# Inverse softmax sums of the third query block made inside the second attention, block 0 normalised ahead of the one-hots, and only the last block inverted in the output stage

## What is computed

```python
xn = _layernorm(x)
x = x + _L0_attn_ref(xn, ...) + _L0_ffn_ref(xn, ...)      # linear attention; 16 experts
xn = _layernorm(x)
x = x + _L1_attn_ref(xn, ...) + _L1_ffn_ref(xn, ...)      # causal windowed softmax attention; routed block
```

```python
attn = jax.nn.softmax(scores, axis=-1)
out = jnp.einsum('bhqk,bhkd->bhqd', attn, v)
return jnp.einsum('bnh,hm->bnm', out, w_out)
```

## Time and profile before

| what | us |
|---|---|
| median of 3 runs (lowest, highest) | 1543.32 (1541.33, 1543.69) |
| the profiled execution, its own time | 1543.52 |
| its span | 1541.8 |
| TensorE busy in it | 1471.3 (95%) |
| VectorE busy | 1029.9 (67%) |
| ScalarE busy | 755.4 (49%) |
| GpSimd busy | 461.0 (30%) |
| mean granted clock of TensorE | 0.981 |

### The profile page before, as it was taken

The page is one execution under the profiler, slowest core; times in us unless marked ns, Lnnn a source line. Parts: engine busy times, 40 slices in busy tenths (PEclk is TensorE's granted clock), DMA queues, the critical chain, the costliest instruction groups (busy, mean ns, idle before and its releaser), DMA issues. The chain is left out here.

```text
span 1541.8 us, 23547 instructions
## 1 busy us (share of the span) xinstructions
PE 1471.3 (95%) x6981; PEld 1062.9 (69%) x6981; DVE 1029.9 (67%) x2939; ACT 755.4 (49%) x1282; POOL 461.0 (30%) x691
## 2 busy tenths in 40 slices
PE   6999999999998999999989999999999998898998
PEld 4778788888776788788855555555555545687776
DVE  5453666666657656887767886665668974578592
ACT  5623556556564544433325555555555562235561
POOL 0000677777610112323221212221212213054062
PEclk9999999999999999999969999999999999999999
DMA  5001222211110334366797405314134017744021
GB/s 185 1 1 70 95 76 75 112 75 75 55 48 7 130 110 125 121 193 197 193 236 282 110 19 120 74 55 120 35 92 120 13 62 208 247 171 155 22 89 14
DMA packets 107124, 161.53 MB, mean 105 GB/s; under 512 B 12352, under 2 KB 63696, under 8 KB 100624
## 3 DMA queue, kind: packets, MB, share of 16 engines
q1 hardware_dynamic: 101868, 153.64, 32.6%
q10 hardware_dynamic: 4516, 5.38, 1.0%
q0 software_dynamic: 640, 1.31, 0.4%
HBM read 117.44 MB, written 42.87 MB: 104 GB/s over the span
## 5 line engine op out<-in xcount | busy, mean ns | idle before, releaser
L2138 ACT ACTIVATE l_pt<-banks 128x1024 f32<-128x1024 f32 (+3 forms) x288 | 218.6, 811 | 140.2 <-PE banks L2013 138.3
L2210 DVE CUSTOM_DVE_ANT_0 stage<-banks,l_edges 128x384 f32<-128x384 f32 (+3 forms) x384 | 201.7, 542 | 73.1 <-issue 71.8
L2050 PE MATMUL banks<-l_pt,l_v 128*64 128x512 f32 (+3 forms) x1152 | 222.0, 507 | 2.0 <-POOL l_pt L2108 2.0
L718 POOL TENSOR_TENSOR ex_hl<-ex_h,ex_hh 128x512 fp32r<-128x512 f32 x128 | 165.6, 1301 | 81.1 <-ACT ex_hh L686 81.0
L2107 POOL TENSOR_TENSOR l_turn<-l_before 128x2 f32<-128x2 f32 x192 | 38.6, 201 | 385.0 <-ACT l_pt L2138 375.4
L751 DVE SCALAR_TENSOR_TENSOR ex_rw<-banks,ex_wb 128x512 f32<-128x512 f32 x128 | 88.3, 691 | 78.9 <-PE banks L75 78.8
L2213 DVE TENSOR_REDUCE l_mx<-banks 128x1 f32<-128x384 f32 (+1 forms) x208 | 113.1, 544 | 39.9 <-PE banks L1991 39.2
L2050 PEld LDWEIGHTS banks<-l_pt,l_v 128*64 128x64 f32 x1152 | 69.3, 138 | 91.4 <-issue 68.2
L686 ACT ACTIVATE ex_hh<-ex_h 128x512 fp32r<-128x512 f32 x128 | 80.9, 632 | 103.6 <-DVE ex_h L759 103.4
L73 PE MATMUL banks<-ex_xlh,ex_wh 128*128 128x512 f32 x256 | 101.7, 397 | 2.0 <-DVE ex_rw L751 2.0
L74 PE MATMUL banks<-ex_xll,ex_wh 128*128 128x512 f32 x256 | 99.8, 390 | 0.0
(11 more groups left out here) (454 smaller groups left out, 3496.9 us busy)
## 6 DMA issues: line engine op xcount, KB each, us to landing
ex_wb<-gates_by_expert SPq DMA_DIRECT2D x16, 1024.0 KB, 4.6
l_v<-layer_v SPq DMA_DIRECT2D x8, 1024.0 KB, 16.9
layer_qk<-qkv_yh SPq DMA_DIRECT2D x30, 256.0 KB, 3.2
layer_qk<-qkv_yl SPq DMA_DIRECT2D x30, 256.0 KB, 3.6
layer_v<-qkv_vs SPq DMA_DIRECT2D x15, 512.0 KB, 5.0
ex_ws<-ew_in SPq DMA_DIRECT2D x16, 384.0 KB, 5.0
l_q<-layer_qk SPq DMA_DIRECT2D x12, 512.0 KB, 7.7
l_k<-layer_qk SPq DMA_DIRECT2D x12, 512.0 KB, 13.3
```

The costliest lines, as they stand in the source:

```text
L718: pool.tensor_tensor(hl[:, k % RING, :], h[:, k % RING, :], raw(hh[:, k % RING, :]), ALU.subtract).then_inc(hl_done, 1)
L2050: last = pe.matmul(bank[h * 2 * HD:(h + 1) * 2 * HD, (qa - b * BT) * P:(qz + 1 - b * BT) * P], v[par][:, kt, h, :], pt[:, step_part(b, j), ...
L2138: act.activation(pt[:, step_part(b, j), :, 0:width], G.banks[:, 2 * slot:2 * slot + 2, 0:width], ACT.Exp, scale=scale).then_inc(p_done, 1)
L2210: dve.tensor_tensor_reduce(cutoff[:, n % 4, 0:width], G.ps[5 + n % MB][:, 0:width], masked, 1.0, NEG, ALU.add, ALU.max, mx[:, h, m, c:c + ...
```

## The change

In the attention's last turn, SyncE waits for the reciprocal, stores the inverses, spreads block 0's and loads block 1's outputs at u = 6 instead of u = 7, ahead of unit 6's store. At u = 7 it loads the sums of block 2 to a new tile `dn2` once unit 6's store has landed, waits for their reciprocal and stores them. VectorE normalises block 0 before the places and one-hots; the one-hots come in four groups of four, with the reciprocal of `dn2` behind the first group and the low parts of block 0 between the others; the chosen numbers come last. ScalarE's copies go two behind steps 6 and 7 and two behind steps 8 and 9. TensorE's picks move from step 8 to step 10, where they stand ahead of the last two value steps.

In the output stage only block 3's sums are loaded and inverted (64 columns per partition in place of 128). SyncE's order becomes: inverses 1, residual 0 and 1, outputs of block 2, wait for the stores, load of the sums, residual 2 and 3, inverses 2, norm vectors, wait for the reciprocal, store of the inverses, residual 4 and 5, outputs of block 3, wait, inverses 3, residual 6 to 15, biases. VectorE waits for the sums and inverts them at tile 3 instead of at the start.

```diff
--- before.py
+++ after.py
@@ -1784,6 +1784,7 @@
     o_out = [G.sem(f"l1_o_out{k}") for k in range(2)]
     den_in, rden, rden_out, z_in, out_o_in, out_o1_in = (
         G.sem("l1_" + n) for n in ("den_in", "rden", "rden_out", "z_in", "out_o_in", "out_o1_in"))
+    den2_in, rden2, rden2_out = (G.sem("l1_" + n) for n in ("den2_in", "rden2", "rden2_out"))
     w_in, w_hi, w_lo, on, ohi = (G.sem("l1_" + n) for n in ("w_in", "w_hi", "w_lo", "on", "ohi"))
     first_in, far_ones = G.sem("l1_first_in"), G.sem("l1_far_ones")
     nm_done, mh_done, cut_done = G.sem("l1_nm"), G.sem("l1_mh"), G.sem("l1_cut")
@@ -1791,7 +1792,7 @@
         "sr_in", "iota", "link", "sel", "pos_mm", "oh", "pick_mm"))
     PR = 4
     LEAD = 37
-    PLACES, PICKS = 4, 8
+    PLACES, PICKS = 4, 10
     MB = 3
     with ExitStack() as stack:
         M = Memory(nc, stack, "l1_")
@@ -1805,7 +1806,7 @@
         wraw = nc.alloc_sbuf_tensor_at("l1_wraw", [P, NC, D], F32, offset=v0_at)
         pt = nc.alloc_sbuf_tensor_at("l1_pt", [P, PR, 2, TB], F32, offset=G.qw_at)
         ob = M.sb("ob", [P, 2, TB])
-        dn = M.sb("dn", [P, 2 * H0 * TB // P])
+        dn, dn2 = M.sb("dn", [P, 2 * H0 * TB // P]), M.sb("dn2", [P, H0 * TB // P])
         sr, junk, same = G.out_o1[:, :, :].rearrange("p g n -> p (g n)"), M.sb("junk", [P, 2, T], BF16), M.sb("same", [P, 2, P])
         count, rank_of, sel = M.sb("count", [P, NT, 6]), M.sb("rank", [P, NT]), M.sb("sel", [P, NT], BF16)
         place, numi, ordi = M.sb("place", [P, NT]), M.sb("numi", [P, NT], I32), M.sb("ordi", [P, SEL], I32)
@@ -1875,13 +1876,17 @@
                     if last and u == NB + 2:
                         sp.wait_ge(o_out[1], 64 * (PAIRS * NB // 2 - 1))
                         sp.dma_start(dn[:, :], sums_of(S.den, 0, 2)).then_inc(den_in, 16)
-                    if last and u == NB + 3:
                         sp.wait_ge(rden, 1)
                         sp.dma_start(sums_of(S.rden, 0, 2), dn[:, :]).then_inc(rden_out, 16)
                         sp.wait_ge(rden_out, 16)
                         spread_inverses(sp, S, 0, G.out_z, z_in)
                         sp.wait_ge(sel_done, 1)
                         sp.dma_start(G.out_o1[:, :, :], S.o[:, TB:2 * TB].rearrange("(g p) t -> p g t", p=P)).then_inc(out_o1_in, 16)
+                    if last and u == NB + 3:
+                        sp.wait_ge(o_out[0], 64 * (PAIRS * NB // 2))
+                        sp.dma_start(dn2[:, :], sums_of(S.den, 2, 3)).then_inc(den2_in, 16)
+                        sp.wait_ge(rden2, 1)
+                        sp.dma_start(sums_of(S.rden, 2, 3), dn2[:, :]).then_inc(rden2_out, 16)
                     if last and u == 2 * NB - 1:
                         G.last_outputs = lambda queue, no=no, pair=i * 2 + par, b=b: store(queue, no, pair, b)
                     else:
@@ -1896,6 +1901,7 @@
             G.o_out = [(o_out[n], 64 * PAIRS * NB // 2) for n in range(2)]
             sp.wait_ge(out_o_in, 16)
             sp.wait_ge(out_o1_in, 16)
+            sp.wait_ge(rden2_out, 16)
 
         assert KEYS % 2 == 0
 
@@ -2171,8 +2177,8 @@
                             output(i - 1, 2 * NB - 1)
                         for at in due(i, position(u, j + 1), last):
                             rows(*at)
-                        if last and u == 2 * NB - 1 and j == len(plans[u % NB].keys) - 2:
-                            for g in range(NC):
+                        if last and u == 2 * NB - 1 and j in (6, 8):
+                            for g in range(j - 6, j - 4):
                                 act.wait_ge(on, g + 1)
                                 act.activation(G.out_oh[:, g, :], G.out_o[:, g, :], ACT.Copy).then_inc(ohi, 1)
                         if last and u == NB + 1 and j < 4:
@@ -2263,11 +2269,13 @@
                 for t, n in todo[upto(position - 1):upto(position)]:
                     rank(t, n)
 
-            def onehots():
+            def places():
 
                 dve.wait_ge(pos_mm, 1)
                 tokens.done(dve.scalar_tensor_tensor(place[:, :], G.ps[6][:, 0:NT], 1.0, sel[:, :], ALU.add, ALU.mult))
-                for t in range(NT):
+
+            def onehots(tiles):
+                for t in tiles:
                     dve.tensor_scalar(onehot[:, t, :], order[:, :], place[:, t:t + 1], None, ALU.is_equal
                                       ).then_inc(oh_done, 1)
 
@@ -2301,15 +2309,21 @@
                         dve.wait_ge(den_in, 16)
                         dve.reciprocal(dn[:, :], dn[:, :]).then_inc(rden, 1)
                     if last and u == 2 * NB - 1:
-                        onehots()
                         dve.wait_ge(z_in, 64)
                         dve.wait_ge(out_o_in, 16)
                         for g in range(NC):
                             dve.tensor_tensor(G.out_o[:, g, :], G.out_z[:, g, :], G.out_o[:, g, :], ALU.mult).then_inc(on, 1)
-                        chosen()
+                        places()
+                        onehots(range(NT // 4))
+                        dve.wait_ge(den2_in, 16)
+                        dve.reciprocal(dn2[:, :], dn2[:, :]).then_inc(rden2, 1)
+                        onehots(range(NT // 4, NT // 2))
                         for g in range(NC):
                             dve.wait_ge(ohi, g + 1)
                             dve.tensor_tensor(G.out_ol[:, g, :], G.out_o[:, g, :], raw(G.out_oh[:, g, :]), ALU.subtract)
+                            if g % 2 == 1:
+                                onehots(range((g + 3) * NT // 8, (g + 5) * NT // 8))
+                        chosen()
 
             looped(dve, PAIRS // 2, body)
 
@@ -2387,7 +2401,7 @@
     BANKS = 6
     with ExitStack() as stack:
         M = Memory(nc, stack, "o1_")
-        dn = M.sb("dn", [P, 2 * H0 * TB // P])
+        dn = M.sb("dn", [P, H0 * TB // P])
         o_at = nc.sbuf_base
         o = [None, G.out_o1] + [M.sb(f"o{b}", [P, NC, TB]) for b in range(2, NB)]
         z = M.sb("z", [P, 2, NC, TB])
@@ -2420,23 +2434,23 @@
             inverses(1)
             residual(0)
             residual(1)
+            values(2)
             for sem, count in G.o_out:
                 sp.wait_ge(sem, count)
-            sp.dma_start(dn[:, :], sums_of(S.den, 2, NB)).then_inc(den_in, 16)
-            sp.wait_ge(rden, 1)
-            sp.dma_start(sums_of(S.rden, 2, NB), dn[:, :]).then_inc(rden_out, 16)
+            sp.dma_start(dn[:, :], sums_of(S.den, NB - 1, NB)).then_inc(den_in, 16)
             residual(2)
             residual(3)
-            values(2)
+            inverses(2)
             sp.dma_start(R.ln[:, 0, :], I["ln1_w"]).then_inc(R.ln_in, 16)
             sp.dma_start(R.ln[:, 1, :], I["ln2_w"]).then_inc(R.ln_in, 16)
-            sp.wait_ge(rden_out, 16)
-            inverses(2)
-            for t in range(BT, 2 * BT):
+            sp.wait_ge(rden, 1)
+            sp.dma_start(sums_of(S.rden, NB - 1, NB), dn[:, :]).then_inc(rden_out, 16)
+            for t in range(BT, BT + 2):
                 residual(t)
             values(3)
+            sp.wait_ge(rden_out, 16)
             inverses(3)
-            for t in range(2 * BT, NT):
+            for t in range(BT + 2, NT):
                 residual(t)
             R.load_biases(sp, I)
 
@@ -2484,10 +2498,11 @@
                 dve.wait_ge(ohi, (b - 1) * NC + g + 1)
                 dve.tensor_tensor(ol[b][:, g, :], o[b][:, g, :], raw(oh[b][:, g, :]), ALU.subtract).then_inc(olo, 1)
 
-            dve.wait_ge(den_in, 16)
-            dve.reciprocal(dn[:, :], dn[:, :]).then_inc(rden, 1)
             for t in range(NT):
                 b, k = t // BT, t % BT
+                if t == BT - 1:
+                    dve.wait_ge(den_in, 16)
+                    dve.reciprocal(dn[:, :], dn[:, :]).then_inc(rden, 1)
                 if b + 1 < NB:
                     normal(b + 1, k)
                 elif k == 0:
```

## The result

| | kernel before | changed kernel |
|---|---|---|
| median, us (14 runs each) | 1543.18 | 1547.29 |
| lowest, highest | 1540.71, 1545.70 | 1540.44, 1552.73 |
| span of the profiled execution | 1541.8 | 1545.2 |
| last unit: places to the output stage's first product | 11.86 | 13.96 |
| output stage: first product to last addition | 58.20 | 61.37 |

The ratio is 1.0028 with a 95% interval of 1.0016 to 1.0040: the changed kernel is 2.5 to 6.2 us slower, 4.3 in the middle. The forecast was +5.0 (1548.3 us, range 1541.0 to 1553.0).

The account below looks back on a forecast made before the run. Transfers were taken as the scarce thing, with TensorE's gaps, ended by VectorE's waits, what could be won. Attention's end +0.8, row 6 +3.5 and clock +0.7 gave +5.0 on 1543.5, or 1548.3 us against the median; range 1541.0 to 1553.0.

Parts of the forecast that it names:

- part 3: Output stage, block 2: residual row 6, queued behind block 3's 2 MB, lands at 1322.4; +3.5 us, bounds +0.2 and +6.2.
- part 4: TensorE's clock after its idle time at the third block: slow products cost +0.7 us, bounds -1.8 and +1.5.
- Part 2: First wait of the output stage: VectorE starts 3 us earlier but waits 3 us for row 2; nothing won at block 1.
- Part 1: Attention's end: earlier inverses, but work between the one-hots and a wait for the third sums; +0.8 us, bounds -0.6 and +2.0.
- (a): Rival, output stage: residual rows 6 and 7 are in time; -4.5 us, so 1538.8 us; chance 0.14.
- point of decision: Output stage: if row 6 has landed by 1315.3, VectorE's cycle alone sets block 2 and the kernel is faster.
- (b): Rival, output stage: block 3's inverses take 3.0 us instead of 5.5, row 6 at 1319.9; it cancels, 1545.0 us; chance 0.24.
- (c): Rival, attention's end: third sums land at 1280, delaying the one-hots and last value steps; +2.0 us, whole 1549.5; chance 0.12.

Follow-up runs that it names:

- first experiment: Changed kernel with only residual tiles 6 and 7 back ahead of block 3's values and inverses; stage 54.63 us, ratio to the kernel before 0.9995.
- second experiment: Changed kernel with only block 2's values back behind the sums and residual tiles 2 and 3; product at -1.77, end 12.08 us, ratio to the kernel before 1.0023.
- rows first with the one-hots together: Changed kernel with residual tiles 6 and 7 ahead of block 3's transfers and all 16 one-hots in one run behind the places; ratio to the kernel before 0.9979.
- the two with batched low parts: Changed kernel, one-hots together, next block's four chunks made at its first tile; rows 6 and 7 ahead of or behind block 3's transfers: 0.9984, 0.9982 of the kernel before.

## Why the prediction was right

**The direction and its cause** (part 3) held: residual row 6, issued behind 2 MB, decides the third block. Forecast: block 2's inverses at 1310.7, row 6 at 1322.4; measured 1310.81 and 1323.45, the stage having started 0.3 us later than the clock of before. The first experiment shows the cause by moving rows 6 and 7 alone. TensorE reached tile 9 not 3.5 but 4.8 us later, counted from the first product: 0.8 from row 6, and 0.5 because the last products of the tile before ran at the low level (0.63 us each in place of 0.40), which I had counted under part 4. In the second execution of each kernel the difference is 2.0 us (37.2 against 35.2). The forecast of 1310.7 has a slip in it: "about 2.0 us earlier" and 1 us for the norm loads make 3.0, so 1311.2, and I wrote 3.5. That it was met within 0.2 us is luck.

**Part 4** was wrong: I set +0.7 us for slow products behind tile 9. Measured from there on it is 20.7 us against 22.3, 1.6 less, at a granted clock of 1.00 against 0.92: the low stretch, which in the kernel before began with tile 9, was over by then. In the second executions it is 22.0 against 22.6. Parts 3 and 4 together, forecast +4.2, were 3.2 in the first pair of executions and 2.9 by the means above.

**Part 2** held in kind: no gain at block 1, a wait for row 2 of 2.8 us (forecast 3). But row 2 came 17.9 us after the first product, not 16.2, and VectorE had its two tiles done 2.0 us later than forecast; the wait has the forecast size because both were late. The low clock of 0.68 that followed was not foreseen. By the second experiment it cost nothing that the timed runs can see, because the wait for row 6 covers it.

**Part 1** was too small: +0.8 forecast, bounds to +2.0, and 2.10 measured. The step that failed is the term "the inverses land by 1273.4", 9.3 us after the reciprocal's end. The store that I took at 1.56 us from the row before took 3.8, and 2.0 to 3.8 over the executions, so the product of block 0 was not done "just as the one-hots can start" but 2 us later. The same late store, ahead in the same queue, also put back the load of the third sums: they released VectorE 4.8 us after the places' first product, where I had 3.2 and an upper bound of 4.6. The new wait for them, forecast as 1.0, is 0.74, since the one-hots ahead of it were late too. Over the six executions the attention's part is about 1.4 us. The rest of this sum was itself too long: with the inverses nearly on time (values late, product at -1.77) the end is 0.2 us longer than before, not 0.8.

**The sum was closer than its terms.** In the first pair of executions part 1 missed by +1.3, part 3 by +1.3 and part 4 by -2.3 us; the forecast of +5.0 against the measured 4.3 owes part of its closeness to that.

**Rivals.** (a), rows in time, is what the first experiment makes of the kernel; its point of decision, 1315.3, was passed by 8 us. (b), broadcast loads as fast as plain ones, fell: row 6 came at 1323.4, not 1319.9. (c), a worse end of the attention, did occur in this execution (+2.10, with the third sums as late as its 1280), but the late sums are not its cause by themselves: removing the wait for them gave 1 us. The upper end of the range, 1553.0, is not what I said of it. Row 6 at its upper bound with the attention's end as forecast gives 1551.0; 1553.0 needs the upper bounds of parts 1 and 4 as well. The median is 1.0 us under the forecast.

## What to carry to other kernels

Where one queue feeds a fixed sequence of steps, list for each step which transfer it needs and what now stands ahead of it: here 256 KB behind 2 MB landed 9.5 us after its issue, and more than the wait removed at the front was given back there. In a moved piece of work look at who waits for it: with the same VectorE work the attention's end was about 2 us shorter when the part that TensorE waits for came first. The best versions here (rows first with the one-hots together, and the two with batched low parts) are at 0.998 of the kernel before. And compare stages over several executions: one pair gave 3.2 us for the output stage, its second executions 1.4.

## What the hardware showed that I had not expected

- The 64 KB store of the first inverses went through in 1.56 us right behind other DMAs of the queue, and needed 2.0 to 3.8 us in the eleven executions where SyncE had issued nothing for 11.7 us. The pause is the same in all eleven, so it can't be what makes 2.0 into 3.8; whether it makes 1.56 into 2.0 wasn't tried.
- Identical code ahead of the last unit puts the places between 1268.9 and 1276.8 us in these executions, nearly 8 us apart. A change of 4 us can't be read from two spans, only from stages.
- The clock behind the stall at block 1: 0.68 granted from 1300 to 1316 in the changed kernel, with its gap of 3.7 us, and full clock in the kernel before, with gaps of 1 us; yet with the old output stage and the changed attention, where the gaps were 0.3 to 1.0 us, tile 5 took 4.1 us instead of 2.8 (granted 0.79 from 1298 to 1314). So short gaps did not keep the clock up in every execution; what decides isn't shown here.
